# A graph network kernel on one core: groups of 4, 4, 4 and 4 tiles instead of 4, 6 and 6, spread side work, and adjacency compares moved from GpSimd to VectorE

## The reference, cut to what matters

```python
h = jnp.maximum(_layernorm(x, axis=-1), 0.0)
A = (adj != 0).astype(x.dtype)
for l in range(weight.shape[0]):                      # 5 layers
    m = jnp.einsum('bnd,de->bne', h, weight[l])
    agg = jnp.einsum('bij,bid->bjd', A, m)
    h = _gru_cell(agg, h, w_ih, w_hh, b_ih, b_hh)
# _gru_cell:
#   r = sigmoid(i_r + h_r); z = sigmoid(i_z + h_z); n = tanh(i_n + r * h_n)
#   return (1.0 - z) * n + z * h
out = x + h * mask[..., None]
```

## Time and profile before

| what | value |
|---|---|
| median of 3 runs | 377.11 us (376.7 to 378.42) |
| the profiled execution | 377.65 us, its span 375.9 us |
| PE busy | 363.5 us, 97% |
| VectorE busy | 310.2 us, 83% |
| ScalarE busy | 297.6 us, 79% |
| GpSimd busy | 275.7 us, 73% |
| TensorE clock granted | 0.996 of full, 2.4 GHz |
| DMA queue of the loads and transposes | 51.7% of 16 engines' span |

### The profile page before, as it was taken

How to read it: one execution, slowest core, us unless ns; L and a number is a source line. 1 busy time by engine, 2 the same in 40 slices (tenths; PEclk the granted TensorE clock), 3 DMA queues, 4 the chain that set the end, 5 groups by cost and what they waited for, 6 DMA issues and landing times.

```text
span 375.9 us, 6545 instructions
## 1 busy us (share of the span) xinstructions
PE 363.5 (97%) x2152; PEld 184.0 (49%) x2152; DVE 310.2 (83%) x572; ACT 297.6 (79%) x495; POOL 275.7 (73%) x258
## 2 busy tenths in 40 slices
PE   7899999999999999999999999999999999999992
PEld 3454555555555544445444545544455545555441
DVE  4879888888878788798989898888878787777775
ACT  5988898998878888798888887687677776677662
POOL 3759779788778979587695876867877655555796
PEclk9999999999999999999999999999999999999998
DMA  8536535747744556745364774327734423287422
GB/s 259 189 58 140 114 74 123 175 95 180 169 111 111 86 94 121 150 87 114 83 115 112 146 192 82 88 58 161 134 70 102 97 56 58 56 228 184 95 84 84
DMA packets 102176, 44.46 MB, mean 118 GB/s; under 512 B 91392, under 2 KB 91776, under 8 KB 102144
## 3 DMA queue, kind: packets, MB, share of 16 engines
q1 hardware_dynamic: 102000, 43.80, 51.7%
q10 hardware_dynamic: 144, 0.26, 0.2%
HBM read 17.57 MB, written 4.19 MB: 58 GB/s over the span
## 4 chain that ended last, share of the span: by engine, by line
PE 79%; DVE 9%; POOL 5%; DMA 2%; issue 2%; SPq 1%; ACT 1%; DVEq 0%; POOLq 0%
PE ps_r L273 8%; PE ps_z L275 8%; PE ps_z L274 8%; PE ps_z L273 8%; PE ps_r L275 8%; PE ps_r L274 8%; PE ps_s L347 4%; PE ps_s L346 4%; PE ps_in L275 4%; PE ps_in L274 4%; PE ps_in L273 4%; PE ps_hn L273 4%; PE ps_hn L275 4%; PE ps_hn L274 4%; DVE ps_in L605 1%
## 5 line engine op out<-in xcount | busy, mean ns | idle before, releaser
L778 POOL TENSOR_TENSOR zh<-z,h 128x512 f32<-128x512 f32 x80 | 101.8, 1272 | 77.3 <-ACT z L461 77.0
L455 ACT ACTIVATE r<-ps_r,b_sum,unscale 128x512 f32<-128x512 f32 x80 | 62.2, 778 | 46.9 <-PE ps_r L275 46.0
L465 ACT ACTIVATE ps_in<-ps_in,b_ih,unscale 128x512 f32<-128x512 f32 x80 | 60.0, 751 | 19.2 <-DVE ps_in L605 17.5
L783 POOL TENSOR_TENSOR hp<-h,hp 128x512 f16<-128x512 f32 x64 | 74.0, 1156 | 1.3 <-ACT hp L471 1.3
L599 DVE SCALAR_TENSOR_TENSOR rhn<-ps_hn,b_hn,r 128x512 f32<-128x512 f32 x80 | 59.9, 749 | 17.1 <-ACT r L455 16.8
L605 DVE TENSOR_TENSOR ps_in<-ps_in,rhn 128x512 f32<-128x512 f32 x80 | 56.0, 699 | 16.0 <-PE ps_in L275 13.7
L611 DVE SCALAR_TENSOR_TENSOR ps_in<-z,ps_in 128x512 f32<-128x512 f32 x79 | 54.6, 691 | 11.0 <-ACT ps_in L465 11.0
L461 ACT ACTIVATE z<-ps_z,b_sum,unscale 128x512 f32<-128x512 f32 x80 | 61.6, 770 | 0.7 <-PE ps_z L275 0.7
L616 DVE TENSOR_TENSOR h<-zh,ps_in 128x512 f32<-128x512 f32 x78 | 53.6, 687 | 10.3 <-POOL zh L778 2.1
L593 DVE TENSOR_TENSOR s_lo<-ps_s,s_hi 128x512 f16<-128x512 f32 x80 | 54.4, 680 | 0.4 <-ACT s_hi L449 0.4
L449 ACT CAST s_hi<-ps_s 128x512 f16<-128x512 f32 x80 | 46.6, 582 | 0.5
(11 more groups left out here) (109 smaller groups left out, 741.3 us busy)
## 6 DMA issues: line engine op xcount, KB each, us to landing
x_in<-in_x SPq DMA_DIRECT2D x16, 256.0 KB, 3.7
adj_in<-in_adj SPq DMA_DIRECT2D x16, 256.0 KB, 3.9
x_out<-in_xT SPq DMA_DIRECT2D x16, 256.0 KB, 3.1
mask_in<-in_mask_row SPq DMA_DIRECT2D x16, 256.0 KB, 3.6
out<-x_out SPq DMA_DIRECT2D x15, 256.0 KB, 2.3
nat<-hp SPq DMA_TRANSPOSE x64, 3.1
fold_in<-in_fold_lhs SPq DMA_DIRECT2D x1, 320.0 KB, 3.9
out<-x_out ACTq DMA_DIRECT2D x1, 256.0 KB, 2.6
```

The source lines that it names most:

```text
L455: nc.scalar.activation(r[:], ps_r[:], ACT.Sigmoid, bias=b_sum[:, 0:1], scale=unscale[:, 0:1]).then_inc(r_done, 1)
L465: nc.scalar.activation(ps_in[K % 2][:], ps_in[K % 2][:], ACT.Tanh, bias=b_ih[:, 2:3], scale=unscale[:, 0:1]).then_inc(n_done, 1)
L778: nc.gpsimd.tensor_tensor(zh[:, K % 2], z[:, K % 2], h[:, t % RING], ALU.mult).then_inc(zh_done, 1)
L783: nc.gpsimd.tensor_tensor(h_lo(t), h[:, t % RING], h_hi(t), ALU.subtract).then_inc(h_lo_done, 1)
```

## The change

The groups become (4, 4, 4, 4): units 0 to 19, 20 to 39, 40 to 59, 60 to 79. All tiles from 4 on go by split, DMA transpose and join; `HALVES` is gone, and with it TensorE's transposes of tiles 4 to 9. The join is made in two halves in two units (stages 8 and 9, so `STAGES` is 10). The adjacency of tiles 4 to 15 is compared by VectorE in stage 7, not by GpSimd in stage 2. Preparation is 3 units apart up to tile 7, then 5 (`SPREAD`). Layer 1 is folded in unit 0 instead of unit 2. The mask product and the final sum of tiles 0 to 11 are done in different units, spread to 5 units apart while tiles are still being prepared. The states of the last group's first three tiles are left in PSUM and multiplied by the mask on VectorE, and `FINISH` is 3.

```diff
-GROUPS = (4, 6, 6)
+GROUPS = (4, 4, 4, 4)
-HALVES = 10
-FINISH = 5
-STAGES = 9
+FINISH = 3
+STAGES = 10
+SPREAD = 5
...
-        gap = 3 if t < starts[1] + GROUPS[1] else 5
+        gap = 3 if t < starts[1] + GROUPS[1] else SPREAD
...
-        ends[t] = soon if t >= starts[-1] or not t else max(soon, ends[t - 1] + 3)
+        if t >= starts[-1]:
+            ends[t] = soon
+        elif t and ends[t - 1] > prep[TILES - 1]:
+            ends[t] = max(soon, ends[t - 1] + 3)
+        else:
+            ends[t] = max(soon, ends[t - 1] + SPREAD if t else 0)
+            ends[t] += (prep[TILES - 1] + 3 - ends[t]) % SPREAD
...
+    adds = {t: ends[t] + (ends[t] + 1 not in ending and ends[t] + 2 < N) for t in ends}
...
                 if K == N - 1:
                     break
+                if K == 0:
+                    fold(1)
                 pe.wait_ge(s_lo_done, K + 1)
...
-                if tile_at_stage[5].get(K, HALVES) < HALVES:
-                    transpose_first(tile_at_stage[5][K])
...
-                if folding(K):
+                if folding(K) > 1:
                     fold(folding(K))
...
-                if K in tile_at_stage[6] and tile_at_stage[6][K] < HALVES:
-                    transposed(tile_at_stage[6][K])
-                if K in tile_at_stage[6] and tile_at_stage[6][K] >= HALVES:
+                if K in tile_at_stage[6]:
                     split(tile_at_stage[6][K])
...
-                out_ap = h[:, t % RING] if K < N - 2 else ps_in[K % 2][:]
+                out_ap = h[:, t % RING] if K < END else ps_in[K % 2][:]
...
+            def join(t, half):
...
+                two = slice(2 * half, 2 * half + 2)
+                state = h[:, t % RING].rearrange("p (g c) -> p g c", g=TG)[:, two].rearrange("p g c -> p (g c)")
+                joined = nc.vector.tensor_copy(state.bitcast(U16).rearrange("p (c b) -> p b c", b=2),
+                                               halves_t[:, t % 2].rearrange("p (b g) c -> p b g c", b=2)[:, :, two].rearrange(
+                                                   "p b g c -> p b (g c)"))
...
-                if tile_at_stage[8].get(K, 0) >= HALVES:
-                    join(tile_at_stage[8][K])
+                if K in tile_at_stage[7]:
+                    adjacency(tile_at_stage[7][K])
+                for half in range(2):
+                    if K in tile_at_stage[8 + half]:
+                        join(tile_at_stage[8 + half][K], half)
...
-                if K == N - 2:
+                if END <= K < N - 1:
                     masked_state(K)
...
-                if K in tile_at_stage[2]:
-                    adjacency(tile_at_stage[2][K])
...
-                if K in ending and K < N - 1:
-                    final(ending[K])
+                if K in ending and ending[K] < starts[-1]:
+                    masked_result(ending[K])
+                if K in adding:
+                    final(adding[K])
```

More of the change, by code:

```diff
@@ L47, in gnn_kernel @@
     at = {u: K for K, u in enumerate(units)}
+    END = at[starts[-1], LAST]
     inner = [sum(l < LAST for _, l in units[:K + 1]) for K in range(N)]
@@ L59, in gnn_kernel @@
         soon = at[t, LAST] + 1
-        ends[t] = soon if t >= starts[-1] or not t else max(soon, ends[t - 1] + 3)
+        if t >= starts[-1]:
[5 more added lines that the diff above has]
+            ends[t] += (prep[TILES - 1] + 3 - ends[t]) % SPREAD
     tile_at_stage = [{prep[t] + s: t for t in prep} for s in range(STAGES)]
     ending = {ends[t]: t for t in ends}
+    adds = {t: ends[t] + (ends[t] + 1 not in ending and ends[t] + 2 < N) for t in ends}
+    adding = {adds[t]: t for t in ends if t < TILES - 2}
+    storing = {adds[t] + 1: t for t in ends}
     fetching = {ends[t] - FETCH: [t] for t in ends}
-    fetching[N - FINISH - FETCH].append(TILES - 1)
+    fetching.setdefault(N - FINISH - FETCH, []).append(TILES - 1)
     xT_t = xT.rearrange("d (t c) -> t d c", c=TILE)
@@ L211, in transpose_halves @@
             def transpose_halves(t):
[L212 to L213 removed]
+                sp.wait_ge(split_done, t - FIRST + 1)
+                if t - FIRST >= 2:
                     sp.wait_ge(h_init, t - 1)
@@ L260, in _ @@
                     transpose_first(tile_at_stage[6][K])
[L261 to L264, removed]
+                    transpose_halves(tile_at_stage[6][K])
+                if K in storing:
+                    store(storing[K])
                 for t in fetching.get(K, ()):
@@ L580, in opposite_mean, with adjacency @@
                                         ALU.mult).then_inc(minus_done, 1)
-            def first_adjacency(t):
-                dve.wait_ge(adj_loaded[t], 16)
-                nc.vector.tensor_scalar(a[:, t], adj_in[:, t], 0.0, None, ALU.not_equal).then_inc(a_done, 1)
+            def adjacency(t):
+                dve.wait_ge(adj_loaded[t % ADJ], 16 * (t // ADJ + 1))
+                if t >= RING:
+                    dve.wait_ge(s_mm, at[t - RING, LAST] + 1)
+                nc.vector.tensor_scalar(a[:, t % RING], adj_in[:, t % ADJ], 0.0, None, ALU.not_equal).then_inc(a_done, 1)
             def transposed_low(t):
@@ L698, in first @@
                 weight_scale()
-                first_adjacency(0)
+                adjacency(0)
                 dve.wait_ge(scale_done, 1)
@@ L709, in first @@
                 s_low(0)
-                first_adjacency(1)
+                adjacency(1)
                 moments(3)
                 aggregate(3)
-                first_adjacency(2)
+                adjacency(2)
                 dve.wait_ge(bias_done, 2)
@@ L724, in _ @@
                 if K == 0:
-                    first_adjacency(3)
+                    adjacency(3)
                 if K in tile_at_stage[0]:
@@ L760, in natural_low @@
                 nc.gpsimd.tensor_tensor(nat_lo(t), h0[:, t % LN], nat_hi(t), ALU.subtract).then_inc(nat_lo_init, 1)
[L762 to L766, removed]
             def kept(K):
@@ L783, in state_low, with masked_result @@
                 nc.gpsimd.tensor_tensor(h_lo(t), h[:, t % RING], h_hi(t), ALU.subtract).then_inc(h_lo_done, 1)
+            def masked_result(t):
+                f = t % FRING
+                pool.wait_ge(ends_loaded[f], 32 * (t // FRING + 1))
+                pool.wait_ge(h_done, at[t, LAST] + 1)
+                nc.gpsimd.tensor_tensor(mask_in[:, f], mask_in[:, f], h[:, t % RING], ALU.mult).then_inc(masked, 1)
             def final(t):
                 f = t % FRING
[L787 to L790, removed]
+                if t < starts[-1]:
                     pool.wait_ge(masked, t + 1)
                 else:
-                    pool.wait_ge(last_masked, 1)
+                    pool.wait_ge(last_masked, t - starts[-1] + 1)
                 nc.gpsimd.tensor_tensor(x_out[:, f], x_out[:, f], mask_in[:, f], ALU.add).then_inc(out_done, 1)
```

16 lines of the change are left out of this document (6 added, 10 removed).

## The result

The changed kernel takes 372.82 us (median of 6 runs, 372.54 to 373.38) against 377.10 us (376.64 to 378.42) for the kernel before on the same chips: a ratio of 0.9884, with a 95% interval of 0.9865 to 0.9903. The forecast was 372.1. The profiled execution took 372.54 us, its span 370.5.

A forecast was written before the change was run, and what follows sets the result against it. TensorE was taken as the bound, 80 units of 4.33 us being an untouched floor of 346.6. Terms -2.64 - 0.65 - 0.48 - 3.33 + 0.44 + 1.6 + 0.05 gave -5.0, so a median of 372.1 us, range 370.0 to 375.8.

The forecast's parts named there:

- The two ends: Units 0 to 3, forecast at -1.13 us, and unit 76 to the last x_out's start, forecast at +0.05.
- the middle: Units 4 to 75: forecast -3.9 us, from -2.64 - 3.33 + 0.44 + 1.6.
- Transposes off TensorE: Tiles 4 to 9: six transposes of 0.44 us leave TensorE, -2.64 us.
- Fold and moments: Units 0 to 3: layer 1's fold into unit 0's idle time, -0.65 us; tile 4's moments leaving unit 1, -0.48.
- Stalls of units 25 to 59: Units 25 to 59: stalls' causes go with halved joins, adjacency off GpSimd and spread products and sums, -3.33 us.
- spacing 5: Tiles 8 to 15: half joins end at +5.10, compares at +5.16, just under the +5.17 limit: 0 us.
- The exceptions after units 37, 57 and 60: Final sum follows zh at once, ending near +4.97, so half join or compare ends late: +0.44 us.
- Crowded units: Units 10 to 19, tiles 4 to 7, spacing 3: overlapping stages make ScalarE and VectorE late, +1.6 us, worst in unit 15.
- Groups of 4: States needed 4 units later, not 6: transposed state lands with 2.1 us to spare, so 0 us.
- The end: Units 76 and 77: masked product moves from GpSimd to VectorE, 0.7 us against 0.4 + 0.1 idle, +0.05 us.
- more port collisions: Rival: half joins take 0.6 us after release or a tie is lost; 373.3 to 376 us, chance 0.20.
- Slower: Rival: state's loop through DMA, every 4 units, grows if landings exceed 5.2 us; 379 to 382 us, chance 0.06.

## Why the prediction was nearly right

The time was within 0.7 us of the forecast, and that is partly luck. The two ends were forecast 1.2 us too good (without the changed kernel's long unit 0), the middle 1.1 us too bad, and the errors cancel.

1. **Transposes off TensorE, -2.64.** Right: unit 9 is at 4.33, and with groups of 4 alone the six are there again at 0.44 each.
2. **Fold and moments, -1.13.** This step failed, at "if unit 2 is still bound by PE". Unit 3 did fall from 4.72 to 4.33 in every profile but those with tile 4's moments in unit 1. Unit 2 stayed at 5.5: it was bound by tile 3's first transpose, whose landing the fold had just covered. The trace of before had a sign of it, on the weight load ahead of unit 2's first h product:

```profile
27.32 0.10 PEld L273 LDWEIGHTS ps_r<-hp,u_hi 128*128 128x128 f16 x1 [0.53 <-DMA hp<-nat]
```

   I had read 0.65 + 0.44 over the floor as TensorE's own work alone, and a busy engine hides a wait of the same length. So 0.39 came of the 1.13. Casting tile 3 earlier gives the other 0.75.
3. **Stalls of units 25 to 59, -3.33**, and 4, **spacing 5, 0.** Right: those units are at 4.33. But the 3.33 had more than one cause. In the kernel before 1.22 of it is in unit 30, where the join waited for the transposed halves, not for the port:

```profile
153.24 0.90 DVE L648 COPY h<-halves_t 128x1024 uint16<-128x1024 uint16 x1 [1.61 <-DMA halves_t<-halves]
```

   Units 25 and 28 hold another 0.9 behind a late `zh`, and the rest, 1.2, is in or next to units with the other five joins. The changed kernel has no wait for the halves. The half joins end 0.32 after release, as I took it, recorded with 1.00 us and not 1.2 to 1.3; six of the eight compares 0.29 after it, not 0.41, so at +5.04. The exceptions after units 37, 57 and 60 cost 0.03, not 0.44; the half join of unit 37 ends at +5.19, since the final sum of that unit started at once behind `zh` and ended at +4.87, 0.1 before my estimate.
5. **Crowded units, +1.6.** Places right (12, 15, 17), size 0.89. The term was mis-sized, for some 0.5 of the 0.7 us by one guess of order at the port. Unit 14's side work in the changed kernel:

```profile
83.46 0.66 DVE L586 TENSOR_SCALAR minus_mean<-mean_var 128x4 f32<-128x4 f32 x1
84.04 0.41 DVE L593 TENSOR_SCALAR a<-adj_in 128x512 f16<-128x512 f32 x1
84.05 0.45 POOL L768 TENSOR_TENSOR var_eps<-mean_var,eps 128x4 f32<-128x4 f32 x1
```

   I had `var_eps` go first and the compare end at +6.1; the compare went directly behind `minus_mean` and ended at +5.81 (84.45, unit 14 starting at 78.64), and GpSimd's short instruction waited (0.45 us instead of 0.20). The same order in unit 11 has the compare end at +5.45, where I had +5.7. The rest is unit 17, behind ScalarE's layernorm half and split: r starts 0.52 late, not 0.78, and 0.05 is lost, not 0.22.
6. **Groups of 4, 0.** Right that `nat` is never waited for. But "0" was not what the groups are worth: with groups of 4, 6, 6 the rest of the change gains nothing. Tiles 4 to 9 are then due in units 20 to 25, and all their preparation falls in units 1 to 24; with groups of 4 tiles 8 and 9 are due 16 units later. I had placed the new stalls with the new table and never priced the old groups with the new parts.
7. **The end, +0.05.** Failed in size: +0.49. In the changed kernel the mask product takes 0.69 us of VectorE ahead of `rhn`, in units 77 and 78. With no hole in between to recover in, the delays add up: `rhn` starts at +1.99 and then at +2.22, against +1.66 in unit 76, and the last unit asks for `s_lo` earlier than a full unit:

```profile
361.59 0.39 PE L284 MATMUL ps_z<-s_hi,v_hi 128*128 128x512 f16 x1 [0.52 <-DVE s_lo L602]
```

Of the rivals, "more port collisions" needed half joins 0.6 after release: it was 0.32. "Slower" was put in the right place and at the wrong price: it closes every 2 units, not 4, so a landing over 5.2 us would have cost twice as often. What stays open is why one `nat` took 5.0 us to land in the kernel with a gap of 4 and one 5.3 with groups of 4, 6 and 6, against 3.1 in the median; loads were in flight beside the first, but I did not take them away one by one.

## What to carry to other kernels

Before an engine's work is moved out of a unit, look for what else that unit waits for underneath: the next limit may stand directly behind the one removed, as tile 3's first transpose did here. In programs with fixed order, price a loop by what its links stand behind on each engine, not only by its own links. And price a change of deadlines (here the group size) together with the side work that it lets move: each alone, as run here, was worth 0 to 0.2%, both together 1.2%.

## What the hardware showed that I had not expected

- Two instructions already queued for VectorE and GpSimd's common port: the VectorE one directly behind another VectorE one went first (84.04 against 84.05), and GpSimd's 0.20 us instruction was recorded with 0.45.
- A half join took 0.44 us alone and ended 0.32 behind `hp`'s end where it had to wait; most of the recorded 1.00 us is waiting.
- After a wait of 2.44 us for `nat` in the kernel with groups of 3, ending at 206.78, TensorE had the lower of its two clocks for a while. Waits of 2.47 and 2.41 us at 276.40 and 296.34 were followed by a granted 1.00, so the length of the last wait alone doesn't decide it. Three stretches of that kernel (us, busy time of each engine, granted clock, DMA share, GB/s):

```profile
203.00:207.00 4.00, 1.56 (x10) 0.61 (x8) 2.54 (x4) 2.18 (x5) 2.96 (x3) 0.92 0.42 68
207.00:210.00 3.00, 3.00 (x15) 1.50 (x14) 0.86 (x2) 1.23 (x3) 0.96 (x1) 0.54 0.00 0
210.00:213.00 3.00, 2.73 (x13) 1.05 (x11) 2.55 (x8) 2.04 (x4) 1.35 (x2) 1.00 0.56 105
```

  A granted 0.54 is mostly 1.2 GHz. One product in that stretch, and one back at 2.4 GHz:

```profile
207.61 0.63 PE L284 MATMUL ps_in<-s_hi,v_hi 128*128 128x512 f16 x1
...
211.28 0.38 PE L284 MATMUL ps_r<-s_hi,v_hi 128*128 128x512 f16 x1
```
